# A sparse block's ReLU values rounded and split in two halves, its transposed results taken out by VectorE

## The chip, the cores and the metric

One Trainium2 chip, one of its cores. The metric is the device time of one execution in microseconds (us). The kernel before takes 928.79 us, the median of 3 runs (927.91 to 933.05).

## What is computed

Two transformer layers over four rows of 512 tokens, 128 features each. In each layer an attention with 16 heads and a feed-forward part stand behind a modulated layer norm, and each is added to x with a gate. Layer 0's feed-forward part is dense over 15 gated experts and a shared one. Layer 1's is sparse, and it alone is touched here. Cut to what matters:

```python
router_probs = softmax(xt @ Wr + br)                 # xt: 2048 tokens x 128
gates, idx = max(router_probs), argmax(router_probs) # one of E = 8 experts per token
xn = (xt - mu) * rsqrt(var + LN_EPS) * ln_g + ln_b
h = relu(einsum('te,td,edf->tf', onehot, xn, W1) + b1[idx])   # f = 512
y = einsum('te,tf,efd->td', onehot, h, W2) + b2[idx]
return y * gates
```

## The kernel before

All five engines run one program each, tied together by semaphores: TensorE (PE), VectorE (DVE), ScalarE (ACT), GpSimd (POOL) and SyncE (SP), which issues most DMAs. Each engine works strictly in the order in which its program is written. The class `Signal` (L84) is a semaphore with a list of keys: `x.by(ins, key)` lets the instruction count it up, `x.wait_ge(engine, key)` makes an engine wait for that count. `apart` (L414) is an empty instruction that holds the waits in front of it. `step` makes VectorE wait for its own instruction.

**The sparse stage.** When layer 1's attention is done, the normed tokens have been scattered to the DRAM tensor `xs`, sorted by expert into blocks of BLK = 256 tokens, each block with one expert. Eight experts with 2048 tokens need at most NBLK = 15 blocks. `block_table` (L1643) works out which block of `xs` and which expert each of the 15 has; SyncE loads all 15 blocks to `xb` (L642). Then the function `expert_blocks` of each engine goes over the blocks n = 0 to 14. A product in full precision is made of three fp32r matmuls: the value is split into a rounded half (`hi`) and the rest (`lo`), and hi x hi, hi x lo, lo x hi are added up in PSUM.

For a block n these steps follow each other, in order of the data:

1. PE `rows_in` (L1305): two transposes of `xb` to the PSUM tile `singles[0]`.
2. ACT `rounded_rows` (L987, L992) applies the norm's scale and shift and rounds to `xt_hi`; DVE `low_rows` (L1667) does the same without rounding (L1672) and subtracts (L1674) to `xt_lo`.
3. POOL (L813 to L820) copies this expert's bias columns to `b_blk` (L819) and its four weight parts, 2048 elements per partition, to `wst[n % 3]` (L820). There are three such buffers, so the copy for block n waits for `y_full` and `yt_ready` of block n - 3 (L816, L817).
4. PE `first_layer` (L1316): twelve matmuls, four chunks c of 128 hidden units times three products (L1326 to L1328), to the PSUM pair `pairs[n % 2]`, which is two banks with two chunks each. It waits for `xl_ready` and `w_here` of block n.
5. ACT `hidden` (L995): four ReLU activations of 128x256 to `hid1` (L1002), and one copy of all four, 128x1024, rounded to `hid1_hi` (L1009).
6. DVE `low_hidden` (L1676): one subtraction of 128x1024 to `hid1_lo` (L1681).
7. PE `second_layer` (L1331): twelve matmuls (L1338 to L1340) that accumulate in `p_o` or `p_m`, alternately.
8. DVE `result` (L1683): adds the bias `b2` to `yt` (L1688), which signals `yt_ready`.
9. PE `rows_out` (L1343): two transposes of `yt` to the PSUM tile `singles[1]` (L1349), signal `z_full`. ACT `result` (L1011): a copy to `yb` (L1016), signal `yb_ready`. SyncE stores `yb` to `xs` (L645).

Behind the last store POOL gathers the results by 16 indirect DMAs (L825), and DVE gates and adds them to x (L1713, L1716).

**The order on each engine**, written out by hand, in turn n of its loop:

- PE (L1355): `rows_in(n+1)`, `first_layer(n)`, `second_layer(n-1)`, `rows_out(n-2)`.
- ACT (L1020): `rounded_rows(n+1)`, `hidden(n)`, `result(n-2)`.
- DVE (L1691): `low_rows(n+1)`, `low_hidden(n)`, `result(n-1)`.
- POOL (L813): the copies for block n.
- SP (L643): the store of block n.

A signal `e_full` stands for the end of all twelve matmuls of step 4, `relu_done` for all four ReLUs, `e_hi` for the rounded copy, `e_lo` for the subtraction: one each for a block.

Of the kernel before, what the change touches and what calls it, by code (L numbers as in the profile page):

```python
# [10 lines left out]
ALU = mybir.AluOpType  # L11
# [28 lines left out]
NBLK = T * NB // 256 + E1 - 1  # L40
# [173 lines left out]
def build(nc, a, out):  # L214
    ctx = ExitStack()
    with ctx:
# [3 lines left out]
        def sig(name, keys):  # L220
            return Signal(sem(name), keys)
# [158 lines left out]
        table_ready = sig("table_ready", [0])  # L380
        xt_full, xh_ready, xl_ready = (sig(n, blocks) for n in ("xt_full", "xh_ready", "xl_ready"))
        w_here = sig("w_here", blocks)
        e_full, relu_done, e_hi, e_lo = (sig(n, blocks) for n in ("e_full", "relu_done", "e_hi", "e_lo"))
        y_full, yt_ready, z_full, yb_ready = (sig(n, blocks) for n in ("y_full", "yt_ready", "z_full", "yb_ready"))
        xb_in, yb_out = [sem(f"xb_in{i}") for i in range(NBLK)], [sem(f"yb_out{i}") for i in range(2)]
        row_done = sig("row_done", list(range(NB)))
# [24 lines left out]
        def r32(ap):  # L411
            return ap.bitcast(F32R)

        def apart(eng):  # L414
            eng.nop(nofuse=True)
# [413 lines left out]
        def _(act):  # L829
# [156 lines left out]
            def expert_blocks():  # L986
                def rounded_rows(n):  # L987
                    xt_full.wait_ge(act, n)
                    if n >= 2:
                        e_full.wait_ge(act, n - 2)  # L990
                    apart(act)
                    xh_ready.by(act.activation(r32(xt_hi[:, n % 2, :]), singles[0][:, 0:BLK], ACT.Identity,  # L992
                                               bias=cols[:, R_LNB:R_LNB + 1], scale=cols[:, R_LNG:R_LNG + 1]), n)

                def hidden(n):  # L995
                    e_full.wait_ge(act, n)
                    w_here.wait_ge(act, n)
                    if n >= 2:
                        e_lo.wait_ge(act, n - 2)
                    apart(act)  # L1000
                    for c in range(4):
                        ins = act.activation(hid1[:, n % 2, c, :], pairs[n % 2][:, c // 2, BLK * (c % 2):BLK * (c % 2) + BLK], ACT.Relu,  # L1002
                                             bias=b_blk[:, n % 3, c:c + 1])
                    relu_done.by(ins, n)
                    relu_done.wait_ge(act, n)
                    if n >= 2:
                        y_full.wait_ge(act, n - 2)
                    apart(act)
                    e_hi.by(act.activation(r32(hid1_hi[:, n % 2, :, :]), hid1[:, n % 2, :, :], ACT.Copy), n)  # L1009

                def result(n):  # L1011
                    z_full.wait_ge(act, n)
                    if n >= 2:
                        act.wait_ge(yb_out[n % 2], 16 * (n // 2))
                    apart(act)
                    yb_ready.by(act.activation(yb[:, n % 2, :, :].rearrange("p t d -> p (t d)"), singles[1][:, 0:BLK],  # L1016
                                               ACT.Copy), n)

                rounded_rows(0)
                for n in range(NBLK + 2):  # L1020
                    if n + 1 < NBLK:
                        rounded_rows(n + 1)
                    if n < NBLK:
                        hidden(n)
                    if n >= 2:
                        result(n - 2)

            for L in range(2):
                for name, b in lead_parts(L):
# [22 lines left out]
        def _(pe):  # L1052
# [251 lines left out]
            def expert_blocks():  # L1304
# [11 lines left out]
                def first_layer(n):  # L1316
                    xl_ready.wait_ge(pe, n)
                    w_here.wait_ge(pe, n)
                    if n >= 2:
                        relu_done.wait_ge(pe, n - 2)  # L1320
                    else:
                        s_taken.wait_ge(pe, (1, NSU - 2 + n))
                    for c in range(4):
                        dst = pairs[n % 2][:, c // 2, BLK * (c % 2):BLK * (c % 2) + BLK]
                        hi, lo = (r32(wst[n % 3][:, half, P * c:P * (c + 1)]) for half in range(2))
                        pe.matmul(dst, hi, r32(xt_hi[:, n % 2, :]), start=True, stop=False)  # L1326
                        pe.matmul(dst, hi, r32(xt_lo[:, n % 2, :]), start=False, stop=False)
                        ins = pe.matmul(dst, lo, r32(xt_hi[:, n % 2, :]), start=False, stop=True)  # L1328
                    e_full.by(ins, n)

                def second_layer(n):  # L1331
                    e_lo.wait_ge(pe, n)
                    if n >= 2:
                        yt_ready.wait_ge(pe, n - 2)
                    dst = (p_o, p_m)[n % 2][:, 0:BLK]
                    for c in range(4):
                        hi, lo = (r32(wst[n % 3][:, 2 + half, P * c:P * (c + 1)]) for half in range(2))
                        pe.matmul(dst, hi, r32(hid1_hi[:, n % 2, c, :]), start=(c == 0), stop=False)  # L1338
                        pe.matmul(dst, hi, r32(hid1_lo[:, n % 2, c, :]), start=False, stop=False)
                        ins = pe.matmul(dst, lo, r32(hid1_hi[:, n % 2, c, :]), start=False, stop=(c == 3))  # L1340
                    y_full.by(ins, n)
# [36 lines left out]
        def _(dve):  # L1378
# [287 lines left out]
            def expert_blocks():  # L1666
                def low_rows(n):  # L1667
                    xh_ready.wait_ge(dve, n)
                    if n >= 2:
                        e_full.wait_ge(dve, n - 2)  # L1670
                    apart(dve)
                    step(dve.tensor_scalar(singles[0][:, 0:BLK], singles[0][:, 0:BLK], cols[:, R_LNG:R_LNG + 1],  # L1672
                                           cols[:, R_LNB:R_LNB + 1], ALU.mult, ALU.add))
                    xl_ready.by(dve.tensor_tensor(r32(xt_lo[:, n % 2, :]), singles[0][:, 0:BLK], xt_hi[:, n % 2, :], ALU.subtract), n)  # L1674

                def low_hidden(n):  # L1676
                    e_hi.wait_ge(dve, n)
                    if n >= 2:
                        y_full.wait_ge(dve, n - 2)
                    apart(dve)  # L1680
                    e_lo.by(dve.tensor_tensor(r32(hid1_lo[:, n % 2, :, :]), hid1[:, n % 2, :, :], hid1_hi[:, n % 2, :, :], ALU.subtract), n)  # L1681

                def result(n):  # L1683
                    y_full.wait_ge(dve, n)
                    if n >= 2:
                        z_full.wait_ge(dve, n - 2)
                    apart(dve)
                    yt_ready.by(dve.tensor_scalar(yt[:, n % 2, :], (p_o, p_m)[n % 2][:, 0:BLK], b_blk[:, n % 3, 4:5], None, ALU.add), n)  # L1688

                low_rows(0)  # L1690
                for n in range(NBLK + 1):  # L1691
                    if n + 1 < NBLK:
                        low_rows(n + 1)
                    if n < NBLK:
                        low_hidden(n)
                    if n >= 1:
                        result(n - 1)

            for L in range(2):
                lead(L)  # L1700
# [47 lines left out]
```

## Time and profile before

| | us |
|---|---|
| median of 3 runs | 928.79 |
| lowest, highest | 927.91, 933.05 |
| the profiled execution, its own time | 935.38 |
| its span, first to last instruction | 933.7 |
| of it: the sparse stage, first block's transposes to last store (829 to 907) | 78 |
| behind it: gather and last addition (907 to 934) | 27 |

| engine | busy us in the span | share |
|---|---|---|
| PE matmul | 781.5 | 84% |
| PE weight load | 491.4 | 53% |
| DVE | 625.7 | 67% |
| ACT | 532.4 | 57% |
| POOL | 246.7 | 26% |

Shares over the whole span say little about the sparse stage, which is a twelfth of it; it has to be read by its own stretch of the trace. "Issue" in a chain or as a releaser is time in which the engine waited for nothing that the profile shows. The start of an instruction minus the start of the one before it is what it occupies its engine for; the duration in a row is somewhat longer, as two neighbours overlap. Matmul ends are modelled.

### The profile page before, as it was taken

The page shows a single profiled execution, that of the slowest core. Times are in us where ns is not written, and L with a number is a line of the kernel's source. Part 1 is how long each engine was busy: PE and PEld are TensorE (multiplying, and loading weights), DVE is VectorE, ACT ScalarE, POOL GpSimd, SP SyncE. Part 2 cuts the span into 40 slices and gives each one's busy share as a digit, 9 for nine tenths or more (in the row PEclk, how much of TensorE's full clock was granted, in tenths as well). Part 3 has the DMA queues.
Part 4 walks back from the last instruction along what each step waited for, and adds up shares of the span by engine and source line. Part 5 has one row for each costly group of instructions (what it writes and reads, how often), then busy time and mean ns, then how long its engine had stood idle before and what let it go on. Part 6 is the DMA issues. An engine that isn't in the chain of part 4 may idle for free.

```text
span 933.7 us, 12907 instructions
## 1 busy us (share of the span) xinstructions
PE 781.5 (84%) x4212; PEld 491.4 (53%) x4212; DVE 625.7 (67%) x1292; ACT 532.4 (57%) x976; POOL 246.7 (26%) x327
## 2 busy tenths in 40 slices
PE   5698878888987999999989889999999998338850
PEld 2454445545544777778767544444444442228740
DVE  3475586776663876866767696798898794435633
ACT  2355445546556677777767446667666665127740
POOL 4247654525422000000000230003202231144425
PEclk9599799999999999999999999999999997759975
DMA  6433311111100870000001121231312310021113
GB/s 177 77 65 89 69 36 21 36 36 35 34 5 1 240 211 0 1 1 1 1 11 23 25 68 35 37 79 30 91 35 43 81 25 13 0 74 46 34 34 85
DMA packets 56622, 46.84 MB, mean 50 GB/s; under 512 B 5830, under 2 KB 46619, under 8 KB 56555
## 3 DMA queue, kind: packets, MB, share of 16 engines
q1 hardware_dynamic: 55291, 43.52, 19.7%
q0 software_dynamic: 1120, 2.30, 0.9%
q8 instruction: 34, 0.56, 0.2%
q10 hardware_dynamic: 144, 0.20, 0.1%
q14 instruction: 33, 0.27, 0.1%
HBM read 14.67 MB, written 14.55 MB: 31 GB/s over the span
## 4 chain that ended last, share of the span: by engine, by line
PE 31%; DVE 8%; ACT 5%; issue 3%; POOL 2%; DMA 1%; POOLq 0%; SPq 0%; ACTq 0%; DVEq 0%
PE single L1193 7%; PE p_o L1210 6%; PE pair L1173 5%; DVE mneg L1582 3%; PE p_m L1076 2%; POOL yg L825 1%; ACT hid L1002 1%; DVE hid_lo L1681 1%; ACT hid_hi L1009 1%; ACT ring L928 1%; PE p_m L1286 1%; PE p_m L1287 1%; PE p_m L1288 1%; PE pair L1255 1%; PE pair L1257 1%
## 5 line engine op out<-in xcount | busy, mean ns | idle before, releaser
L928 ACT ACTIVATE ring<-single 128x512 f32<-128x512 f32 (+3 forms) x512 | 252.8, 518 | 193.6 <-PE single L1193 185.8
L1582 DVE TENSOR_REDUCE mneg<-pair 128x2 f32<-128x1024 f32 (+3 forms) x256 | 258.3, 1022 | 70.3 <-PE pair L1177 33.8
L1193 PE MATMUL single<-q_op,k_op 128*128 128x512 f32 (+3 forms) x512 | 216.9, 443 | 13.8 <-ACT ring L928 8.8
L1173 PE MATMUL pair<-k_op,q_op 128*128 128x512 f32 (+3 forms) x512 | 166.8, 404 | 16.9 <-DVE mneg L1582 11.3
L1193 PEld LDWEIGHTS single<-q_op,k_op 122*128 122x128 f32 (+1 forms) x512 | 97.6, 197 | 96.2 <-ACT ring L928 73.1
L1173 PEld LDWEIGHTS pair<-k_op,q_op 120*128 120x128 f32 (+1 forms) x512 | 97.6, 202 | 57.4 <-DVE mneg L1582 34.7
L1210 PE MATMUL p_o<-ring,vaug 128*9 128x512 f32 (+3 forms) x1024 | 115.6, 524 | 1.0 <-ACT ring L928 0.9
L1634 DVE TENSOR_TENSOR ring<-ring,single 128x1024 f32<-128x1024 f32 x60 | 73.3, 1221 | 47.1 <-ACT ring L957 45.6
L957 ACT ACTIVATE ring<-pair,cols 128x512 f32<-128x512 f32 x136 | 86.1, 685 | 32.7 <-PE pair L1257 27.5
L1639 DVE TENSOR_TENSOR hid_lo<-ring,hid_hi 128x1024 fp32r<-128x1024 f32 x68 | 83.3, 1225 | 23.1 <-ACT hid_hi L972 20.0
L972 ACT ACTIVATE hid_hi<-ring 128x1024 fp32r<-128x1024 f32 x68 | 72.2, 1062 | 31.7 <-issue 30.6
L731 POOL TENSOR_SCALAR_AFFINE_SELECT ring<-ring 128x256 f32<-128x256 f32 x128 | 52.3, 409 | 137.0 <-ACT ring L928 136.7
L767 POOL MEMSET k_op<- 128x2048 f32 x2 | 3.6, 1807 | 223.0 <-PE p_m L1288 223.0
L1255 PE MATMUL pair<-h,w 128*128 128x512 f32 x136 | 56.1, 412 | 0.0
L1257 PE MATMUL pair<-h,w 128*128 128x512 f32 x136 | 53.8, 396 | 0.0
L1256 PE MATMUL pair<-h,w 128*128 128x512 f32 x136 | 53.8, 395 | 0.0
L784 POOL TENSOR_TENSOR h_tok<-xn,tabs 128x512 f32<-128x512 f32 x4 | 5.1, 1276 | 153.7 <-DVE xn L1416 153.7
L1681 DVE TENSOR_TENSOR hid_lo<-hid,hid_hi 128x1024 fp32r<-128x1024 f32 x15 | 19.0, 1269 | 29.0 <-ACT hid_hi L1009 29.0
L1210 PEld LDWEIGHTS p_o<-ring,vaug 128*9 128x9 f32 x1024 | 15.3, 89 | 32.9 <-issue 19.6
L794 POOL DMA_INDIRECT xs<-xn,idx x16 | 15.7, 983 | 63.4 <-DVE idx L1559 42.5
L1002 ACT ACTIVATE hid<-pair,b_blk 128x256 f32<-128x256 f32 x60 | 23.5, 476 | 13.7 <-PE pair L1328 13.7
L1175 PE MATMUL pair<-bfc,id_bf 128*128 128x128 bf16 x128 | 31.3, 245 | 0.0
(313 smaller groups left out, 1319.8 us busy)
## 6 DMA issues: line engine op xcount, KB each, us to landing
xs<-zero SPq DMA_DIRECT2D x10, 1024.0 KB, 10.3
k_op<-hl SPq DMA_DIRECT2D x112, 64.0 KB
q_op<-hl SPq DMA_DIRECT2D x16, 256.0 KB
stage<-in_L_ffn_W_dram SPq DMA_DIRECT2D x8, 512.0 KB, 5.0
stage<-in_L_ffn_rW_dram SPq DMA_DIRECT2D x6, 512.0 KB, 5.0
q_op<-hl SPq DMA_DIRECT2D x48, 64.0 KB
xb<-xs SPq DMA_DIRECT2D x15, 128.0 KB, 2.0
xs<-yb SPq DMA_DIRECT2D x15, 128.0 KB, 1.7
```

Of the source, the lines that this page charges most:

```text
L928: exp_done.by(act.activation(ring[:, n % 8, lo:T], singles[n % 2][:, lo:T], ACT.Exp), (L, n))
L957: ins = act.activation(ring[:, k + c, :], pairs[v % 2][:, c, :], ACT.Gelu, bias=cols[:, R_B0 + 2 * u + c:R_B0 + 2 * u + c + 1])
L972: g_hi.by(act.activation(r32(hid_hi[:, i % 2, :, :]), ring[:, k:k + 2, :], ACT.Copy), i)
L1173: ins = pe.matmul(both[:, i, 0:hi], r32(qs[:, P * qt:P * (qt + 1)]), r32(ks[:, 0:hi]), start=i == 0 or L == 1 or qt >= 2, stop=L == 1)
L1193: st_full.by(pe.matmul(singles[n % 2][:, lo:T], r32(ks[:, P * kc:P * (kc + 1)]), r32(qs[:, lo:T]), start=True, stop=True), (L, n))
L1210: ins = pe.matmul(p_o[32 * j:32 * j + HD + 1, lo:T], vaug[:, (NB * L + G // NG) % 2, kc, GH * (G % NG) + j, :], ring[:, (GH * Q + j) % 8, ...
L1255: pe.matmul(pairs[v % 2][:, c, :], hi, r32(h[:, r, 0, :]), start=True, stop=False)
L1256: pe.matmul(pairs[v % 2][:, c, :], hi, r32(h[:, r, 1, :]), start=False, stop=False)
L1257: ins = pe.matmul(pairs[v % 2][:, c, :], lo, r32(h[:, r, 0, :]), start=False, stop=True)
L1582: s_taken.by(dve.tensor_reduce(mneg[:, G % 2, 2 * p:2 * p + 2, qt], both[:, :, 0:hi], axis=AX.X, op=ALU.max, negate=True), (L, m))
L1634: gated.by(dve.tensor_tensor(both, both, singles[1][:, :].unsqueeze(1).broadcast_to([P, 2, T]), ALU.mult), v)
L1639: g_lo.by(dve.tensor_tensor(r32(hid_lo[:, i % 2, :, :]), ring[:, k:k + 2, :], hid_hi[:, i % 2, :, :], ALU.subtract), i)
```

## The change

- `e_full`, `relu_done`, `e_hi` and `e_lo` get two keys for each block, (n, 0) and (n, 1).
- PE `first_layer` signals `e_full` behind the sixth and the twelfth matmul, so at each full bank of the pair.
- ACT `hidden` waits for each half by itself, makes its two ReLUs, and rounds in two instructions of 128x512 in place of one of 128x1024. It makes all four ReLUs before the first rounding; the wait for `relu_done` before each rounding is for that half.
- DVE `low_hidden` subtracts in two instructions of 128x512, each behind its own `e_hi`.
- PE `second_layer` waits for `e_lo` (n, 0) before chunk 0 and for (n, 1) before chunk 2.
- The copy of `singles[1]` to `yb` leaves ACT (`result`, an activation with Copy) and goes to DVE (`rows_out`, a `tensor_copy`) as the last step of a turn, behind `result(n-1)`; its waits, for `z_full` and for the store that last read the buffer, go with it.

```diff
-        e_full, relu_done, e_hi, e_lo = (sig(n, blocks) for n in ("e_full", "relu_done", "e_hi", "e_lo"))
+        halves = [(n, i) for n in blocks for i in range(2)]
+        e_full, relu_done, e_hi, e_lo = (sig(n, halves) for n in ("e_full", "relu_done", "e_hi", "e_lo"))
...
                 def hidden(n):
-                    e_full.wait_ge(act, n)
                     w_here.wait_ge(act, n)
                     if n >= 2:
-                        e_lo.wait_ge(act, n - 2)
-                    apart(act)
-                    for c in range(4):
-                        ins = act.activation(hid1[:, n % 2, c, :], pairs[n % 2][:, c // 2, BLK * (c % 2):BLK * (c % 2) + BLK], ACT.Relu,
-                                             bias=b_blk[:, n % 3, c:c + 1])
-                    relu_done.by(ins, n)
-                    relu_done.wait_ge(act, n)
+                        e_lo.wait_ge(act, (n - 2, 1))
+                    for i in range(2):
+                        e_full.wait_ge(act, (n, i))
+                        apart(act)
+                        for c in range(2 * i, 2 * i + 2):
+                            ins = act.activation(hid1[:, n % 2, c, :], pairs[n % 2][:, i, BLK * (c % 2):BLK * (c % 2) + BLK], ACT.Relu,
+                                                 bias=b_blk[:, n % 3, c:c + 1])
+                        relu_done.by(ins, (n, i))
                     if n >= 2:
                         y_full.wait_ge(act, n - 2)
-                    apart(act)
-                    e_hi.by(act.activation(r32(hid1_hi[:, n % 2, :, :]), hid1[:, n % 2, :, :], ACT.Copy), n)
-
-                def result(n):
-                    z_full.wait_ge(act, n)
-                    if n >= 2:
-                        act.wait_ge(yb_out[n % 2], 16 * (n // 2))
-                    apart(act)
-                    yb_ready.by(act.activation(yb[:, n % 2, :, :].rearrange("p t d -> p (t d)"), singles[1][:, 0:BLK],
-                                               ACT.Copy), n)
+                    for i in range(2):
+                        relu_done.wait_ge(act, (n, i))
+                        apart(act)
+                        e_hi.by(act.activation(r32(hid1_hi[:, n % 2, 2 * i:2 * i + 2, :]), hid1[:, n % 2, 2 * i:2 * i + 2, :], ACT.Copy), (n, i))
...
                         ins = pe.matmul(dst, lo, r32(xt_hi[:, n % 2, :]), start=False, stop=True)
-                    e_full.by(ins, n)
+                        if c % 2:
+                            e_full.by(ins, (n, c // 2))
...
                 def second_layer(n):
-                    e_lo.wait_ge(pe, n)
...
                     for c in range(4):
+                        if c % 2 == 0:
+                            e_lo.wait_ge(pe, (n, c // 2))
...
                 def low_hidden(n):
-                    e_hi.wait_ge(dve, n)
                     if n >= 2:
                         y_full.wait_ge(dve, n - 2)
-                    apart(dve)
-                    e_lo.by(dve.tensor_tensor(r32(hid1_lo[:, n % 2, :, :]), hid1[:, n % 2, :, :], hid1_hi[:, n % 2, :, :], ALU.subtract), n)
+                    for i in range(2):
+                        e_hi.wait_ge(dve, (n, i))
+                        apart(dve)
+                        part = slice(2 * i, 2 * i + 2)
+                        e_lo.by(dve.tensor_tensor(r32(hid1_lo[:, n % 2, part, :]), hid1[:, n % 2, part, :], hid1_hi[:, n % 2, part, :],
+                                                  ALU.subtract), (n, i))
...
+                def rows_out(n):
+                    z_full.wait_ge(dve, n)
+                    if n >= 2:
+                        dve.wait_ge(yb_out[n % 2], 16 * (n // 2))
+                    apart(dve)
+                    yb_ready.by(dve.tensor_copy(yb[:, n % 2, :, :].rearrange("p t d -> p (t d)"), singles[1][:, 0:BLK]), n)
+
                 low_rows(0)
-                for n in range(NBLK + 1):
+                for n in range(NBLK + 2):
                     if n + 1 < NBLK:
                         low_rows(n + 1)
                     if n < NBLK:
                         low_hidden(n)
-                    if n >= 1:
+                    if 1 <= n <= NBLK:
                         result(n - 1)
+                    if n >= 2:
+                        rows_out(n - 2)
```

The other lines of the diff name the half (n - 2, 1) where before they named block n - 2, and end ACT's loop at NBLK.

## Rows read from the trace of the kernel before

**Rows 1.** Stretches: us, busy PE PEld DVE ACT POOL, PEclk, DMA: stage, ten blocks.

```profile
829.00:907.00 78.00, 59.45 (x420) 54.40 (x420) 38.69 (x60) 50.73 (x105) 25.90 (x25) 0.89 0.16 50
851.08:894.39 43.31, 36.26 (x278) 33.17 (x279) 25.39 (x41) 33.25 (x70) 20.24 (x20) 1.00 0.10 31
```

**Rows 2.** Waits, 829 to 907: who waited for whom, us in total, times, longest.

```profile
POOL b_blk L819 <- DVE yt L1688: 39.4, 12, 12.3
```

**Rows 3.** Timeline of one turn: start us, us, engine line op tiles xcount [idle before].

```profile
852.87 1.57 ACT L1002 ACTIVATE hid<-pair,b_blk 128x256 f32<-128x256 f32 x4 [1.60 <-PE pair L1328]
854.54 1.06 ACT L1009 ACTIVATE hid_hi<-hid 128x1024 fp32r<-128x1024 f32 x1
855.74 1.23 DVE L1681 TENSOR_TENSOR hid_lo<-hid,hid_hi 128x1024 fp32r<-128x1024 f32 x1 [2.36 <-ACT hid_hi L1009]
856.88 0.48 DVE L1688 TENSOR_SCALAR yt<-p_m,b_blk 128x256 f32<-128x256 f32 x1
857.56 0.19 POOL L819 COPY b_blk<-b_cols 128x5 f32 x1 [2.88 <-DVE yt L1688]
857.69 1.89 POOL L820 CAST wst<-w 128x2048 fp32r x1
857.85 0.42 DVE L1674 TENSOR_TENSOR xt_lo<-single,xt_hi 128x256 fp32r<-128x256 f32 x1
859.68 0.36 PE L1326 MATMUL pair<-xt_hi,wst 128*128 128x256 f32 x1 [0.53 <-issue]
861.25 0.19 POOL L819 COPY b_blk<-b_cols 128x5 f32 x1 [1.68 <-DVE yt L1688]
861.47 1.57 ACT L1002 ACTIVATE hid<-pair,b_blk 128x256 f32<-128x256 f32 x4 [1.46 <-PE pair L1328]
```

**Rows 4.** Timeline: two subtractions beside weight copies.

```profile
849.09 1.89 POOL L820 CAST wst<-w 128x2048 fp32r x1
850.50 1.56 DVE L1681 TENSOR_TENSOR hid_lo<-hid,hid_hi 128x1024 fp32r<-128x1024 f32 x1 [0.81 <-ACT hid_hi L1009]
859.42 1.24 DVE L1681 TENSOR_TENSOR hid_lo<-hid,hid_hi 128x1024 fp32r<-128x1024 f32 x1 [1.14 <-ACT hid_hi L1009]
```

**Rows 5.** Timeline of PE without a stall: first layer, second layer.

```profile
851.08 0.36 PE L1326 MATMUL pair<-xt_hi,wst 128*128 128x256 f32 x1 [0.54 <-issue]
852.58 0.28 PE L1338 MATMUL p_m<-hid_hi,wst 128*128 128x256 f32 x1
```

**Rows 6.** Groups by form, whole span: busy us, mean ns, idle before.

```profile
L1002 ACT ACTIVATE hid<-pair,b_blk 128x256 f32<-128x256 f32 x60 | 23.5, 476 | 13.7 <-PE pair L1328 13.7
L907 ACT ACTIVATE h<-hF 128x512 fp32r<-128x512 f32 x4 | 2.5, 620 | 0.0
L1716 DVE TENSOR_TENSOR x<-x,yg 128x512 f32<-128x512 f32 x4 | 2.8, 691 | 0.1
L1384 DVE COPY cols<-p_m 128x85 f32<-128x85 f32 x1 | 0.2, 248 | 0.0
```

**Rows 7.** Timeline of the first blocks.

```profile
833.38 0.41 PE L1328 MATMUL pair<-xt_hi,wst 128*128 128x256 f32 x1
835.19 1.57 ACT L1002 ACTIVATE hid<-pair,b_blk 128x256 f32<-128x256 f32 x4 [2.02 <-PE pair L1328]
848.28 0.48 DVE L1688 TENSOR_SCALAR yt<-p_m,b_blk 128x256 f32<-128x256 f32 x1
```

**Rows 8.** Busy time by stretch: block 0's second layer; the dense stage.

```profile
839.30:842.20 2.90, 2.90 (x14) 2.90 (x15) 1.95 (x3) 1.58 (x3) 0.00 (x0) 0.51 0.34 101
500.00:520.00 20.00, 20.00 (x88) 15.83 (x87) 15.40 (x13) 15.14 (x20) 0.00 (x0) 1.00 0.02 7
```

**Rows 9.** Timeline and chain of the last block.

```profile
894.39 0.36 PE L1326 MATMUL pair<-xt_hi,wst 128*128 128x256 f32 x1 [1.05 <-issue]
900.31 0.39 PE L1338 MATMUL p_o<-hid_hi,wst 128*128 128x256 f32 x1 [2.62 <-DVE hid_lo L1681]
902.98 0.48 DVE L1688 TENSOR_SCALAR yt<-p_o,b_blk 128x256 f32<-128x256 f32 x1 [2.33 <-PE p_o L1340]
905.21 1.71 DMA xs<-yb
```

More of the change, by code:

```diff
@@ L989, in rounded_rows @@
                     if n >= 2:
-                        e_full.wait_ge(act, n - 2)
+                        e_full.wait_ge(act, (n - 2, 1))
                     apart(act)
@@ L995, in hidden @@
                 def hidden(n):
-                    e_full.wait_ge(act, n)
                     w_here.wait_ge(act, n)
                     if n >= 2:
-                        e_lo.wait_ge(act, n - 2)
-                    apart(act)
-                    for c in range(4):
-                        ins = act.activation(hid1[:, n % 2, c, :], pairs[n % 2][:, c // 2, BLK * (c % 2):BLK * (c % 2) + BLK], ACT.Relu,
-                                             bias=b_blk[:, n % 3, c:c + 1])
-                    relu_done.by(ins, n)
-                    relu_done.wait_ge(act, n)
+                        e_lo.wait_ge(act, (n - 2, 1))
[6 more added lines that the diff above has]
+                        relu_done.by(ins, (n, i))
                     if n >= 2:
                         y_full.wait_ge(act, n - 2)
-                    apart(act)
-                    e_hi.by(act.activation(r32(hid1_hi[:, n % 2, :, :]), hid1[:, n % 2, :, :], ACT.Copy), n)
-                def result(n):
-                    z_full.wait_ge(act, n)
-                    if n >= 2:
-                        act.wait_ge(yb_out[n % 2], 16 * (n // 2))
-                    apart(act)
-                    yb_ready.by(act.activation(yb[:, n % 2, :, :].rearrange("p t d -> p (t d)"), singles[1][:, 0:BLK],
-                                               ACT.Copy), n)
+                    for i in range(2):
+                        relu_done.wait_ge(act, (n, i))
+                        apart(act)
+                        e_hi.by(act.activation(r32(hid1_hi[:, n % 2, 2 * i:2 * i + 2, :]), hid1[:, n % 2, 2 * i:2 * i + 2, :], ACT.Copy), (n, i))
                 rounded_rows(0)
-                for n in range(NBLK + 2):
+                for n in range(NBLK):
                     if n + 1 < NBLK:
                         rounded_rows(n + 1)
[L1023 to L1026, printed above, removed]
+                    hidden(n)
             for L in range(2):
@@ L1319, in first_layer @@
                     if n >= 2:
-                        relu_done.wait_ge(pe, n - 2)
+                        relu_done.wait_ge(pe, (n - 2, 1))
                     else:
@@ L1669, in low_rows @@
                     if n >= 2:
-                        e_full.wait_ge(dve, n - 2)
+                        e_full.wait_ge(dve, (n - 2, 1))
                     apart(dve)
```

## The prediction

> **What bounds the kernel now.** I read the busy times by stretch first. The sparse stage is 78.0 us long, and ten of its fifteen blocks take 43.31 us between two starts of the first layer, 4.33 each, with PE busy for 36.26 and ACT for 33.25 [rows 1]. No engine is full, so a loop of waits bounds the stage.
>
> The chain of waits puts most of the stage down to the ReLUs, the rounding and the subtraction, but before every second first layer it shows PE idle for 0.53 with "issue" as the releaser [rows 3]. That is a wait which the profile couldn't name. The table of waits and the timeline name it. POOL's copy of a block's weights waits for `yt` all 12 times that it can, 39.4 us in all [rows 2], and PE's first layer starts 0.10 after the copy ends (857.69 + 1.89 = 859.58, then 859.68) [rows 3]. VectorE makes that `yt`, which belongs to the block before, only behind this block's subtraction. So the loop is, from block n's ReLUs: 1.67 to the rounding, 1.20 to the subtraction, 1.14 to `yt`, 0.81 to the weight copy, 1.89 for it, 0.10 to the first layer of block n+2, 1.79 to its ReLUs. The sum is 8.60, and 861.47 - 852.87 is 8.60 [rows 3]. Even and odd blocks each run such a loop, hence 4.30 a block.
>
> A second thing is in the timeline. The subtraction has two inputs in SBUF and is 1.23 long when POOL is quiet. Where it started at 850.50 under a weight copy that ended at 850.98 it took 1.56 and ended at 852.06, 1.08 behind the copy [rows 4]. The one at 859.42 ended at 860.66, again 1.08 behind the copy of rows 3. One more of the fifteen was stretched in the same way; POOL's copy was 1.89 throughout. So a subtraction can't get further under a weight copy than if it had begun 0.15 before the copy's end.
>
> **The change part by part.**
>
> *First layer and ReLUs by halves.* Twelve matmuls take 1.50 [rows 5], so a half is signalled about 0.72 earlier: first layer to first ReLU becomes 1.79 - 0.72 = 1.07. The ReLUs overlap: (1.57 - 0.48) / 3 = 0.365 from start to start, 0.48 being a single one [rows 3, 6]. The second half's matmuls end about when the third ReLU may start, so the four keep 1.57.
>
> *Rounding in halves.* The first half's ReLUs are done long before, so the rounding needn't wait for the last one and starts at 4 x 0.365 = 1.46, not 1.67. A half's price isn't shown for this tile: 0.53 (half of 1.06) from below, 0.62 from an SBUF copy of 128x512 [rows 6] from above. I take 0.60 long, 0.50 apart. With the 0.14 of the hand-over that rows 3 show, the first subtraction may start at 1.46 + 0.60 + 0.14 = 2.20.
>
> *Subtraction in halves.* Half of 1.23 is 0.62; a 128x512 one took 0.69 [rows 6]. I take 0.69; the whole one occupies 1.14 of its 1.23, so a half occupies 0.60. The second half starts at 2.80 (its input is there at 2.70), `yt` at 3.40, where before it was 4.01 behind the ReLUs.
>
> The loop is then 1.07 + 3.40 + 0.81 + 1.89 + 0.10 = 7.27 for two blocks, 3.64 a block. **But the weight copy now stands in the way.** It runs from 0.81 to 2.70 behind each `yt`; the next block's first half can't count as begun before 2.55, the second follows at 3.15, the next `yt` at 3.75. That is more than 3.64, so I take 3.75 a block. The same sum with the whole subtraction gives 2.55 + 1.14 = 3.69, which is the short step of the kernel before (`b_blk` at 857.56 and at 861.25 [rows 3], with the subtraction of rows 4 in between).
>
> The Trainium skill ("SBUF — State Buffer", section "Who interferes with whom") says that a VectorE instruction with two SBUF inputs and a GpSimd one that reads SBUF exclude each other, and the later one blocks fully. By that rule the half would run its whole length behind the copy, so a block would be about 0.26 longer (an estimate), some 4.0, and the change would give 2.6 less; the trace agrees that the two collide, but shows 1.08 left of 1.23.
>
> *The copy to `yb` on VectorE.* On ACT its removal gives nothing by itself: ACT was idle 1.60 and 1.46 before the ReLUs of this loop [rows 3]. On VectorE it costs between 0.25 (85 columns from PSUM) and 0.48 (`yt`, 256 columns from PSUM) [rows 3, 6]; I take 0.40. It is queued behind `yt`, with the next block's norm and subtraction behind it. `xt_lo` was done 1.39 behind `yt` (858.27) and will be at 1.8, when the weight copy still has 0.9 to run. So the weight copy hides it; were that cover gone, ten blocks would pay 4.0. Its new wait on `z_full` is over some 1.7 earlier, as PE's transposes out follow second layer n-1 directly; the store that it waits for is two blocks old, about 7.5. SP's stores and POOL's copies move with it and are not lengthened. PE's own work, 3.63 a block [rows 1], fits in 3.75, closely.
>
> *The start.* Half of block 0's first layer is done at 833.8 [rows 7], so its first two ReLUs go before 835.19; the roundings start at 835.92 and 836.42, the subtractions at 836.65 and 837.25, the second layer behind the first of them (0.69 and a hand-over) at 837.4. Before, it ran from 839.3 to 842.2 at a granted clock of 0.51, the lower level of 1.2 GHz, behind an idle PE [rows 8]; now there is next to no gap, and I take the upper level, which PE had reached. `xt_lo` of block 2 comes at 838.8, its first layer at 839.1. Block 1: ReLUs 837.4 (ACT comes from block 2's norm), subtraction 839.56, `yt` 840.76, weight copy 841.57 to 843.46. Block 2: subtraction ready at 842.5, held to 843.31, `yt` at 844.51, where it was 848.28 [rows 7]. **Gain 3.8.**
>
> *Ten blocks.* 43.31 against 37.5. **Gain 5.8.**
>
> *The end.* From the last first layer to the last store's landing it was 905.21 + 1.71 - 894.39 = 12.53 [rows 9]. Now the last second layer starts at 1.07 + 2.20 + 0.74 = 4.0 (it was 900.31 - 894.39 = 5.92), takes 1.8 to `yt` at the upper clock (it was 2.67, largely at the lower one, behind 2.62 of idle PE; now the gap is about 0.8), and 3.7 more (it was 3.94). That is 9.5. **Gain 3.0.**
>
> The sum is 12.6. The profiled execution takes 935.38 with a span of 933.7, 6.6 over the median of the runs; it would become 922.8, the span 921.1. All that is saved lies in a stage that both have, so I take the same 12.6 from the median: 928.79 - 12.6 = 916.2.
>
> **The rivals.**
>
> *The halves slip past the weight copy.* If a short subtraction isn't held as the long one was, the waits' loop of 7.27 rules: 36.4 for ten blocks, 0.8 more at the start, so 14.5 in all, 914.3. For it: only few rows show the hold. Against it: two of them end 1.08 behind the copy to the hundredth. Chance 0.13.
>
> *The hand-overs eat the halves.* If each added wait drains its engine, the second half and `yt` start 0.23 later each (0.69 + 0.14 in place of 0.60): 4.2 a block, 1.2 for ten, some 3.3 at the start and 2.6 at the end, 7 in all, 921.8. Against it: `yt` started 0.09 before the subtraction ended, with a satisfied wait and an `apart` between them [rows 3]. Chance 0.10, nearly half of it lost in what can't be told from no change.
>
> *Slower: PE's clock.* PE would be busy for 3.63 of every 3.75. If the chip then grants the lower level through the stage, a layer with its transposes takes the 2.90 of block 0's second layer [rows 8], and a block of two layers some 6.0: with 1.7 more for each of fifteen blocks, 25 slower, 954. It decides as soon as a block takes over 4.6, that is when the lower level holds for a good part of the blocks. Against it: in the dense stage PE is busy 20.00 of 20.00 at a granted clock of 1.00 [rows 8], and the ten blocks now run at 1.00 [rows 1]. Chance 0.05.
>
> **How the numbers follow.** My forecast has 0.72, and 916.2. Its unknown prices move it from 915 (halves at their lower bounds, upper clock everywhere) to 919 (4.0 a block, or the lower clock at the start and the end, 1 us each). With the first two rivals and the scatter of a median of runs that lie 5 apart, the range is 912.5 to 921.8. A measurement here can tell about 0.5%, 4.6 us, from no change. Faster by more: 0.88 (0.70 + 0.13 + 0.05). Within it: 0.07. Slower: 0.05.
>
> **What would show it.** Right: first layers 3.75 apart from block 4 on, with no long and short step in turn; the first half of the subtraction longer than the second, ending 0.54 behind a weight copy; PE's first layer still 0.1 behind the end of a weight copy; block 0's second layer at a granted clock of 1.00; ACT idle longer than before; the last store landing near 894. Wrong: steps under 3.7 with equal halves (first rival), gaps between the halves on VectorE with no weight copy beside them (second), a granted clock of 0.5 in the middle of the stage (third), or VectorE idle in front of its copy to `yb`, waiting for PE, which would break the sum at the cover that I gave that copy.

## The result and the profile after

| | us |
|---|---|
| kernel before, median of 4 runs (lowest to highest) | 928.35 (927.83 to 933.05) |
| changed kernel, median of 4 runs (lowest to highest) | 915.89 (914.68 to 916.99) |
| ratio, 95% interval | 0.986 (0.9828 to 0.9892) |
| profiled execution of the changed kernel: time, span | 916.05, 914.1 |

The change gives 12.5 us, 1.4%; 916.2 was forecast. Two later measurements of the same pair gave 8.0 and 10.0 (experiments 8 and 11). The spans of the two profiled executions differ by more, 933.7 - 914.1 = 19.6. Of that, 9.15 lies ahead of the sparse stage: its first transposes start at 829.27 before and at 820.12 after, though nothing ahead of them was changed. In other profiled executions of kernels of this study they start anywhere from 821 to 829. So the stage is compared by its own clock, from here on: from those first transposes (T0) to the first `yt`, to the last `yt`, and to the start of the gather behind the last store.

The table of waits of the changed kernel, 829 to 896:

```profile
POOL b_blk L820 <- DVE yt L1685: 30.3, 12, 10.9
ACT hid L1004 <- DVE hid_lo L1677: 9.6, 12, 1.5
PE pair L1318 <- issue: 4.2, 12, 0.8
```

POOL still waits for `yt` before all 12 weight copies, 30.3 us where it was 39.4 [rows 2]. In the second line the releaser is misnamed: the ReLUs of block n wait for the subtraction of block n - 2, over long before, and for PE's first half. In this kernel that half and the running subtraction happen to end together; in experiment 3, where they don't, the ReLUs start 1.14 behind the first layer (856.94 - 855.80) and 0.67 before the subtraction ends. The busy times of nine blocks and of block 0's second layer (us; busy of PE, PEld, DVE, ACT, POOL; PE clock; DMA):

```profile
838.22:872.12 33.90, 31.57 (x252) 29.70 (x253) 28.14 (x55) 27.75 (x64) 18.22 (x18) 1.00 0.11 36
828.20:831.00 2.80, 2.77 (x22) 2.66 (x23) 2.04 (x4) 2.80 (x8) 0.00 (x0) 1.00 0.34 105
```

Nine blocks in 33.90 are 3.77 each, where ten took 4.33 each [rows 1]. PE was busy 84% of the time [rows 1] and is now at 93%. VectorE went from 0.59 (25.39 / 43.31) to 0.83. The second row is where PE ran at the lower level before [rows 8].

One turn of the loop, from the timelines of the engines put together in order of time:

```profile
854.25 0.47 DVE L1685 TENSOR_SCALAR yt<-p_o,b_blk 128x256 f32<-128x256 f32 x1
854.65 0.41 DVE L1692 COPY yb<-single 128x256 f32<-128x256 f32 x1
854.98 0.54 DVE L1666 TENSOR_SCALAR single<-single,cols 128x256 f32<-128x256 f32 x1
855.05 1.89 POOL L821 CAST wst<-w 128x2048 fp32r x1
855.55 0.42 DVE L1668 TENSOR_TENSOR xt_lo<-single,xt_hi 128x256 fp32r<-128x256 f32 x1
856.58 1.51 DVE L1677 TENSOR_TENSOR hid_lo<-hid,hid_hi 128x512 fp32r<-128x512 f32 x2 [0.60 <-ACT hid_hi L1012]
857.05 0.36 PE L1318 MATMUL pair<-xt_hi,wst 128*128 128x256 f32 x1 [0.24 <-issue]
858.01 0.47 DVE L1685 TENSOR_SCALAR yt<-p_m,b_blk 128x256 f32<-128x256 f32 x1
858.17 1.57 ACT L1004 ACTIVATE hid<-pair,b_blk 128x256 f32<-128x256 f32 x4 [0.68 <-DVE hid_lo L1677]
859.61 1.16 ACT L1012 ACTIVATE hid_hi<-hid 128x512 fp32r<-128x512 f32 x2
```

Read it as three links. The weight copy starts 0.80 behind `yt` (855.05 - 854.25) and ends at 856.94. The two subtraction halves end at 856.58 + 1.51 = 858.09, 1.15 behind the copy. `yt` starts 0.08 before that. 0.80 + 1.89 + 1.15 - 0.08 = 3.76, and the two `yt` are 3.76 apart. PE's first layer starts 0.11 behind the copy's end, as before, but no longer sets the pace (experiment 3). From the same timelines, a pair at block 0 with no weight copy beside it, the pair of block 2, and a first half alone with the weight copy before it:

```profile
827.49 1.29 DVE L1677 TENSOR_TENSOR hid_lo<-hid,hid_hi 128x512 fp32r<-128x512 f32 x2 [2.34 <-ACT hid_hi L1012]
833.38 2.12 DVE L1677 TENSOR_TENSOR hid_lo<-hid,hid_hi 128x512 fp32r<-128x512 f32 x2 [0.34 <-ACT hid_hi L1012]
858.82 1.90 POOL L821 CAST wst<-w 128x2048 fp32r x1
860.34 0.92 DVE L1677 TENSOR_TENSOR hid_lo<-hid,hid_hi 128x512 fp32r<-128x512 f32 x1 [0.60 <-ACT hid_hi L1012]
```

The pair is 1.29 long when POOL is quiet, 1.51 in a turn, and 2.12 where its input came early. The first half alone ends at 861.26, 0.54 behind the copy's end at 860.72. That is how an engine held by another looks in a profile: no wait, no "issue", only an instruction that is longer than its equals.

The end of the stage, from the chain of waits (start, us, what):

```profile
880.32 0.36 PE p_o L1332
882.12 0.17 DVE yt L1685
882.52 0.42 DVE yb L1692
883.08 0.43 PE single L1343 x2
883.63 0.44 DVE yb L1692
884.19 3.14 DMA xs<-yb
887.87 1.00 POOL yg L826
```

The last first layer starts at 876.19. The last store takes 3.14, where it took 1.71 [rows 9].

### The profile page after: what moved, and what is told of

It reads as the page before. It is cut to its first block and busy times, and to the rows that moved or that the text cites. A ratio compares the mean times of both kernels' runs of the same rounds, so it can differ in the third digit from the quotient of the medians.

```text
span 914.1 us, 12982 instructions
## 1 busy us (share of the span) xinstructions
PE 766.9 (84%) x4212; PEld 483.1 (53%) x4212; DVE 634.3 (69%) x1322; ACT 527.9 (58%) x976; POOL 246.6 (27%) x327
## 5 line engine op out<-in xcount | busy, mean ns | idle before, releaser
L1185 PE MATMUL single<-q_op,k_op 128*128 128x512 f32 (+3 forms) x512 | 213.4, 435 | 14.6 <-ACT ring L929 9.3
L1165 PE MATMUL pair<-k_op,q_op 128*128 128x512 f32 (+3 forms) x512 | 162.9, 396 | 17.3 <-DVE mneg L1576 12.0
L1165 PEld LDWEIGHTS pair<-k_op,q_op 120*128 120x128 f32 (+1 forms) x512 | 94.9, 197 | 58.0 <-DVE mneg L1576 32.9
L1202 PE MATMUL p_o<-ring,vaug 128*9 128x512 f32 (+3 forms) x1024 | 113.4, 515 | 1.0 <-ACT ring L929 0.9
L1677 DVE TENSOR_TENSOR hid_lo<-hid,hid_hi 128x512 fp32r<-128x512 f32 x30 | 23.0, 804 | 11.6 <-ACT hid_hi L1012 10.1
L1167 PE MATMUL pair<-bfc,id_bf 128*128 128x128 bf16 x128 | 30.3, 236 | 0.0
```

Source lines behind the costliest of these rows:

```text
L1165: ins = pe.matmul(both[:, i, 0:hi], r32(qs[:, P * qt:P * (qt + 1)]), r32(ks[:, 0:hi]), start=i == 0 or L == 1 or qt >= 2, stop=L == 1)
L1185: st_full.by(pe.matmul(singles[n % 2][:, lo:T], r32(ks[:, P * kc:P * (kc + 1)]), r32(qs[:, lo:T]), start=True, stop=True), (L, n))
L1202: ins = pe.matmul(p_o[32 * j:32 * j + HD + 1, lo:T], vaug[:, (NB * L + G // NG) % 2, kc, GH * (G % NG) + j, :], ring[:, (GH * Q + j) % 8, ...
```

## The experiments

Each is measured beside the kernel before on the same chip: 1 to 4 on one chip, 5 to 8 on a second, 9 to 12 on a third. In total time the variants of the changed kernel lie so close together that most of their intervals overlap; they are told apart by the stage. "Steps" are the times between two starts of `yt`. Experiments 3, 4, 7 and 12 share one preparation, four weight buffers in place of three, and as many buffers for the bias columns (room was free behind `h` and in the last 1 KB of `at_op`).

### 1. Only the copy to `yb`, on the kernel before

The first two lines are ACT's loop, the last two VectorE's, where the copy follows `yt` of block n - 1.

```diff
-                    if n >= 2:
-                        result(n - 2)
...
+                    if n >= 2:
+                        rows_out(n - 2)
```

> The kernel before, with only the copy to yb moved from ACT to VectorE. Theory (the loop through ReLUs, rounding, subtraction, yt and the weight copy sets the stage, and a weight copy holds up a subtraction): neither ACT's time nor the 0.4 us on VectorE is in the loop, since the copy lies under the weight copy, so within 1 us of the kernel before and still about 8.6 us for two blocks. Rival 1 (ACT's load counts): 15 x 0.26 us = 4 us faster. Rival 2 (VectorE's queue counts, the copy pushes norm and subtraction back): 0.33 us a block, 5 us slower.

Measured: 928.46 (12 runs) against 929.06 (17 runs), ratio 1.0 (0.9984 to 1.0015). The steps are 4.05 and 4.55 in turn, 8.61 for two blocks against 8.60. The copy gives nothing and costs nothing.

Its profile holds something else. Block 0's second layer ran at the upper clock although PE had been idle longer in front of it (2.36) than in the kernel before (2.10):

```profile
833.33 0.39 PE L1327 MATMUL p_o<-hid_hi,wst 128*128 128x256 f32 x1 [2.36 <-DVE hid_lo L1670]
```

And the busy times of that stretch:

```profile
833.33:835.50 2.17, 2.17 (x18) 2.17 (x19) 1.21 (x3) 1.72 (x4) 0.00 (x0) 1.00 0.41 118
```

So the lower level at the start of the profile before [rows 8] wasn't a property of that kernel, but of that execution.

### 2. Only the halves

The changed kernel with the `yb` copy back on ACT.

> The changed kernel, with the copy to yb back on ACT, so the halves alone. Theory: all of the gain is in the halves; ACT has 0.6 us idle in each block, so the same as the changed kernel within 1 us (about 916), 3.77 us from one first layer to the next. Rival (the copy had to leave ACT, as its wait for PE's transposes would stand in front of the next block's norm): 0.2 to 0.4 us a block more, 3 to 6 us slower than the changed kernel.

Measured: 917.73 (915.89 to 921.57), ratio 0.9892 (0.9869 to 0.9916). The steps are 3.77 and the stage from first to last `yt` is 50.57 against 50.47. The halves are the whole of the change.

### 3. Four weight buffers

```diff
-                if n >= 3:
-                    y_full.wait_ge(pool, n - 3)
-                    yt_ready.wait_ge(pool, n - 3)
+                if n >= 4:
+                    y_full.wait_ge(pool, n - 4)
+                    yt_ready.wait_ge(pool, n - 4)
```

> The changed kernel with a fourth weight buffer, so that the weight copy for block n waits for block n-4 and is out of the loop of waits; each copy still starts about 0.8 us behind a yt. Theory (the hold): the subtraction's second input waits for the weight copy whatever block that copy is for, so 3.77 us a block stay and the time is within 1 us of the changed kernel (916). Rival (the loop of waits through the weight copy alone sets the time, the hold costs nothing): PE becomes the bound at about 3.5 us a block, 12 blocks x 0.25 = 3 us faster, 913.

Measured: 918.72 (917.34 to 923.92), ratio 0.9901 (0.9877 to 0.9924). The steps stay at 3.77. In the timeline of a turn:

```profile
854.57 1.89 POOL L822 CAST wst<-w 128x2048 fp32r x1
855.41 2.20 DVE L1678 TENSOR_TENSOR hid_lo<-hid,hid_hi 128x512 fp32r<-128x512 f32 x2
857.53 0.47 DVE L1686 TENSOR_SCALAR yt<-p_o,b_blk 128x256 f32<-128x256 f32 x1
```

Everything ahead of the subtraction is earlier (PE's first layer starts at 855.80, 0.66 before the weight copy that runs then has ended, so it doesn't wait for it), it has no idle time in front of it, and all of that goes into its length, 2.20. It ends at 857.61, again 1.15 behind the copy (856.46). With the first layer's wait for weights gone and the pace the same, the hold is shown to be the bound of the changed kernel.

### 4. The weight copy started earlier

Experiment 3, with POOL's copy released by the end of a subtraction:

```diff
+                    e_lo.wait_ge(pool, (n - 2, 1))
```

> As the one with four buffers, and the weight copy for block n waits also for the second half of the subtraction of block n-2 (e_lo), so it starts about 0.45 us behind yt's start in place of 0.8 and is over before the next subtraction. Theory (the hold): the next subtraction is no longer held, about 3.5 us a block (then PE's own work is the bound), 12 x 0.25 = 3 us faster than the changed kernel, 913. Rival (no hold, the waits alone): no faster than the one with four buffers, both 913 or both 916.

Measured: 914.73 (912.8 to 917.22), ratio 0.9858 (0.9836 to 0.9879). Run once more as experiment 9:

> The kernel with the early copy again, beside the changed kernel on the same chip. Theory: 3.51 us a block in place of 3.77 and one step of 2.9 at the start, 3.5 us faster than the changed kernel. Rival (the part of the runs that stands before the sparse stage differs by more than that between programs): no difference that the intervals show.

914.92 (912.36 to 917.78), ratio 0.9851 (0.9816 to 0.9885). The steps are 3.48 and 3.54 in turn:

```profile
854.00 1.90 POOL L823 CAST wst<-w 128x2048 fp32r x1
855.83 1.29 DVE L1679 TENSOR_TENSOR hid_lo<-hid,hid_hi 128x512 fp32r<-128x512 f32 x2 [0.61 <-ACT hid_hi L1014]
```

The copy ends at 855.90, the subtraction starts 0.07 before that and is 1.29 long: not held any more. What bounds the pace now is not PE's own work, as my expectation had it: experiment 12 runs at 3.31. It is the loop through the weight copy, at its new release point. PE's first layer again starts 0.10 behind the copy's end, at 856.00. From one end of a subtraction to that of two blocks later it is 0.43 to the weight copy, 1.90 for it, 0.10 to the first layer, 1.13 to the ReLUs, 1.44 to the rounding, 0.73 to the subtraction and 1.29 for it: 7.02, or 3.51 a block.

### 5. Halves without the early signal

```diff
-                        if c % 2:
-                            e_full.by(ins, (n, c // 2))
+                        if c == 3:
+                            e_full.by(mid, (n, 0))
+                            e_full.by(ins, (n, 1))
```

`mid` is the matmul before the last. The ReLUs thus wait for the whole first layer, as before the change.

> The changed kernel, but both halves of e_full are signalled only at the end of the first layer (by the last two matmuls), so rounding and subtraction are in halves and the ReLUs start as late as before. Theory: the ReLUs come 0.55 to 0.6 us later, the loop of waits is 7.30 + 0.57 = 7.87 us for two blocks, more than the hold's 2 x 3.77, so 3.93 us a block, and 0.16 x 12 + 1 at start and end = 3 us slower than the changed kernel. Rival (the early signal is worth nothing, since the hold or the weight copy sets the time anyway): the same as the changed kernel.

Measured: 921.82 (920.01 to 923.27), ratio 0.9931 (0.9904 to 0.9957). The steps are 3.81 and 4.09 in turn, 3.95 in the mean, where the loop of waits gave 3.93.

### 6. The early signal without the halves behind it

ReLUs by halves, rounding and subtraction whole.

> The changed kernel, but the rounding and the subtraction are whole again (128x1024) and the ReLUs still go by halves. Theory: yt comes 4.01 us behind the ReLUs in place of 3.38, the loop is 1.12 + 4.01 + 2.80 = 7.93 us for two blocks, 3.97 us a block, 0.20 x 12 + 1 to 2 at start and end = 4 us slower than the changed kernel. Rival (the split of rounding and subtraction only helps PE, whose second layer may start sooner, and PE isn't the bound): the same as the changed kernel.

Measured: 921.29 (920.41 to 922.76), ratio 0.9919 (0.9895 to 0.9943). The steps are 3.82 and 4.05 in turn, 3.94 in the mean, where the loop of waits gave 3.97. In the middle of the stage of both experiments no subtraction is stretched (1.29 the pair, 1.23 the whole one), so there the loop alone sets the pace. In total time neither can be told from the changed kernel of experiment 8 on the same chip (920.36); in the steps they can. Each half of the change alone gives about two thirds of its 0.54 a block (4.31 to 3.95 or 3.94). Both together give less than the sum, 0.54 in place of 0.73, since the hold catches them at 3.77.

### 7. The weight copy a block ahead

Experiment 3 with five buffers for the bias columns, and POOL's copy of block n released by `e_lo` of block n - 3, a full block earlier than in experiment 4.

> Four weight buffers and five for the bias columns; the weight copy for block n waits for the end of the subtraction of block n-3 (and for the second layer of block n-4), so it lies right behind a subtraction, as in the one with the early copy, but is a block ahead of its need. Theory: neither the weight copy nor the hold is in a loop any more; PE's own work (about 3.4 us a block) is the bound where the early copy left 3.51; 12 x 0.08 = 1 us faster than that one and 4 us faster than the changed kernel. Rival (the early copy was already at PE's bound): the same as the early copy, 3.5 us a block.

Measured: 917.62 (913.85 to 920.94), ratio 0.9877 (0.985 to 0.9904). Run once more as experiment 10:

> The kernel with the copy a block ahead again, beside the changed kernel. Theory: PE is the bound at 3.47 us a block, 4 us faster than the changed kernel and within 1 us of the early copy. Rival: as for the early copy.

916.39 (913.07 to 920.92), ratio 0.9866 (0.9832 to 0.9901). The medians lie 2.9 and 1.5 above those of the early copy (the first on another chip), where 1 us below was expected, but the intervals overlap. From first to last `yt` it is 0.6 faster. The steps are 3.47:

```profile
854.29 0.47 DVE L1688 TENSOR_SCALAR yt<-p_o,b_blk 128x256 f32<-128x256 f32 x1
854.80 1.89 POOL L824 CAST wst<-w 128x2048 fp32r x1
856.16 1.68 DVE L1680 TENSOR_TENSOR hid_lo<-hid,hid_hi 128x512 fp32r<-128x512 f32 x2
```

The hold is back: the pair is 1.68 long and ends at 857.84, 1.15 behind the copy (856.69). The same sum gives the pace: 0.51 from `yt` to the copy, 1.89, 1.15, less 0.08, is 3.47. PE is busy 34.73 of 35.00 from 845 to 880, and 35.00 of 35.00 from 838 to 873, and I first read that as PE being the bound. Experiment 12 shows that it wasn't; its waits were only too short to leave gaps between matmuls whose ends are modelled. The starts show them: the transposes of the next block start 0.35 behind those of `yt`, and the first layer 0.17 behind them, where in experiment 12 it is 0.22 and 0.14. The 0.16 between the two sums is the 0.16 between the steps.

### 8 and 11. The changed kernel again, beside the others

> The changed kernel itself, beside the others on the same chip: 0.986 of the kernel before, as in its first measurement; first layers 3.77 us apart.

> The changed kernel again, to be compared with the others of this call: 9 to 12 us under the kernel before; first layers 3.77 us apart.

Measured: 920.36 (916.86 to 923.74) against 928.38, ratio 0.9914 (0.989 to 0.9938); and 919.06 (914.62 to 921.17) against 929.03, ratio 0.9889 (0.9856 to 0.9922). So the gain is 8.0 and 10.0 here, after 12.5 in the first measurement. The stage is the same to 0.1 from first to last `yt` in all three profiled executions (50.47, 50.53, 50.50). So the scatter of the medians seems to lie outside of the stage, or in its end; only one execution of each is profiled, and the others aren't seen.

### 12. The weight copy on top of the subtraction

Experiment 7 with another release. It was made to bring out the hold at its worst: POOL's copy starts when the subtraction does.

```diff
-                    e_lo.wait_ge(pool, (n - 3, 1))
+                    e_hi.wait_ge(pool, (n - 3, 0))
```

> As the copy a block ahead, with one wait moved: the weight copy starts with the first half of a subtraction (it waits for that block's first e_hi) in place of behind its end. It is still a block ahead of its need. Theory (the hold): the second half of each subtraction can't end before the copy does, yt comes 1.5 to 1.8 us later, the loop through the norm's subtraction becomes the bound, about 4.1 us a block, some 7 us slower than the copy a block ahead. Rival (only the loop of waits through the weight copy ever counted): 3.47 us a block, no difference.

Measured: 915.41 (908.87 to 917.57), ratio 0.9856 (0.9818 to 0.9894). The expectation fell, with its sign: the steps are 3.31, the shortest of the study. The timeline of a turn:

```profile
854.32 0.36 PE L1321 MATMUL pair<-xt_hi,wst 128*128 128x256 f32 x1
854.32 1.29 DVE L1680 TENSOR_TENSOR hid_lo<-hid,hid_hi 128x512 fp32r<-128x512 f32 x2 [0.37 <-ACT hid_hi L1015]
854.53 0.54 POOL L823 COPY b_blk<-b_cols 128x5 f32 x1 [0.46 <-ACT hid_hi L1015]
855.01 2.37 POOL L824 CAST wst<-w 128x2048 fp32r x1
857.28 0.38 PE L1346 MATMUL single<-cst,yt 128*128 128x128 f32 x2
857.49 0.38 PE L1308 MATMUL single<-cst,xb 128*128 128x128 f32 x2
857.63 1.29 DVE L1680 TENSOR_TENSOR hid_lo<-hid,hid_hi 128x512 fp32r<-128x512 f32 x2 [0.37 <-ACT hid_hi L1015]
```

The busy times of ten blocks:

```profile
838.00:871.00 33.00, 33.00 (x281) 33.00 (x281) 28.96 (x61) 30.94 (x71) 25.28 (x18) 1.00 0.12 41
```

Now POOL's instructions are the long ones. Its small copy takes 0.54 in place of 0.19 and its weight copy 2.37 in place of 1.89, while the pair keeps its 1.29. So the collision works in both directions: of the two, the one that started first runs on, and the later one pays. The step that failed in my expectation was that POOL's copy would get in between the two halves and hold the second. The small copy did end near the boundary of the halves (855.07), but the weight copy was 0.48 longer (2.37 - 1.89), most of the 0.60 that the pair still had to run, and POOL has that much to spare: it is done at 857.38, 0.25 before the next pair. At 3.31 PE's matmuls follow one another without an idle bracket, PE is busy 33.00 of 33.00, and the starts leave no gap as they do in experiment 7. I take this as PE's bound for the stage; no run here tried for less.

### The stage in all versions

From the starts of the instructions in each profiled execution: T0 to the first `yt`, from there to the last, from there to the gather, and the sum.

```
version                           T0-yt0  yt0-yt14  yt14-gather   sum   step
before                             13.01    60.70      4.20      77.91  3.70/4.90
1  copy to yb only                 12.96    58.57      4.32      75.85  4.05/4.55
5  no early signal                 12.04    52.94      5.08      70.06  3.81/4.09
6  no halves behind the ReLUs      12.21    54.21      4.32      70.74  3.82/4.05
2  halves only                     11.53    50.57      3.73      65.83  3.77
the change                         11.53    50.47      5.75      67.75  3.77
8  the change                      11.53    50.53      4.03      66.09  3.77
11 the change                      11.50    50.50      4.22      66.22  3.77
3  four buffers                    11.52    49.50      6.06      67.08  3.77
4  copy earlier                    11.52    46.73      4.42      62.67  3.48/3.54
9  copy earlier                    11.53    46.75      4.04      62.32  3.48/3.55
7  copy a block ahead              11.55    46.14      5.46      63.15  3.47
10 copy a block ahead              11.44    46.13      5.74      63.31  3.47
12 copy on top                     11.53    44.06      4.04      59.63  3.31
```

The last version is the best of all: its stage is 6.5 shorter than that of the changed kernel in experiments 8 and 11, and its median is 3.7 below that of experiment 11, on the same chip. In total time the two can't be told apart surely, since their intervals against the kernel before overlap (0.9818 to 0.9894, and 0.9856 to 0.9922); in the stage they can.

## Why the prediction was right

*The loop before.* Held. With the halves the pace falls by 0.54 a block, and with one part of them taken away the same loop gave 3.93 and 3.97 ahead of experiments 5 and 6, which ran at 3.95 and 3.94. In experiment 3, where the first layer no longer waits for weights, the pace is no longer tied to that loop.

*The floor under the new loop.* This step decides the size, and it held. My waits' sum gave 3.64 a block and the hold 3.75; measured were 3.77, with the half ending 0.54 behind the copy, as forecast, and the pair 1.15. The first rival, that short halves slip past, is out. The Trainium skill ("SBUF — State Buffer", section "Who interferes with whom") says that such a pair contends for a shared path, that the path is locked for one of them at a time, and that issue order decides who blocks; the words "fully blocks" stand there for VectorE's two-port modes. The order is shown in both directions, by experiments 3 and 12. In length the measurement decides: the held half ended 0.54 behind the copy, not its full 0.69, so that about 0.15 of it lay beside the copy; why, no run shows. My estimate by the rule, some 4.0 a block, doesn't come out of my own terms: 2.70 + 0.60 + 0.60 behind `yt` is 3.90, so 0.15 more than 3.75 and not 0.26. The 3.77 measured is below both. No term of the forecast rests on it.

*The price of a half.* 0.69 was taken for a subtraction and 1.29 for the pair: 1.29 was measured. ReLU to rounding was 1.44 (1.46 taken) and first layer to ReLU 858.17 - 857.05 = 1.12 (1.07 taken). The second rival, hand-overs that eat the halves, is out.

*The copy to `yb`.* Taken at 0.40 and hidden; it is 0.41 long and its removal from the change moves nothing (experiment 2). In the changed kernel its cover is the weight copy: `xt_lo` is done at 855.97, and by the prediction's rule the subtraction couldn't begin to count before 856.79, 0.15 ahead of the copy's end.

*PE's clock.* 1.00 in the nine blocks at 93% busy. The slower rival is out.

*The start.* 3.8 forecast, 3.7 measured: from T0 to the second `yt` is 19.01 before and 15.30 after. But part of it is luck. Some 1.1 of it is the lower clock of block 0's second layer in the profile before (839.29 to 841.97, against 833.33 to 834.87 in experiment 1), and there the idle time was longer. Against experiment 1, whose T0 to second `yt` is 12.96 + 4.55 = 17.51, the gain at the start is 2.2.

*Ten blocks.* 5.8 forecast; the first layers of blocks 4 and 14 are 876.19 - 838.22 = 37.97 apart, so 5.3. Nine steps are 3.77, the tenth 4.07. There POOL's small copy starts 0.97 behind `yt` and not 0.67, the same 0.30 for which the kernel before has a 4.01 among its short steps. I hadn't asked why the last step of the stretch was odd.

*The end.* 3.0 forecast, 1.4 measured: 887.33 - 876.19 = 11.14, where it was 12.53. My terms were 4.0, 1.8 and 3.7. Measured: 4.13 to the second layer, 1.80 to `yt`, 2.07 to the store's issue and 3.14 for the store. Only the store is off. With the 1.71 of experiment 8 the last term is 3.78.

*The sum.* By the profiled executions 3.7 + 5.3 + 1.4 = 10.4, or 11.8 with an ordinary store, against 12.6. The medians say 12.5, 8.0 and 10.0 in three measurements. So 916.2 met 915.89 a little better than the terms deserve: the profile before held a lower clock at its start and a longer end (last `yt` step 2.81 against 2.09 in experiment 1), and I took what it showed as the kernel's. The stage of experiment 1 less that of experiment 11 is 9.6, and for me that is the best value of the gain, though it is one execution against one. The path was right; that the total came out within 0.4 us was in part luck.

*Of the things to look for*, two were off. I wrote that ACT would be idle longer. It is busy 27.75 of 33.90, 82%, against 77% before, and idle 0.68 ahead of its ReLUs, where it was 1.46 and 0.23 in turn. ACT's copy, 0.36 to 0.38 long in the kernel before, was gone, but the block itself became 0.56 shorter. And the last store was to land near 894, by the clock of the profile before, so 65 behind T0; it landed at 887.33, 67.2 behind T0, of which 1.4 is the long store. The first changed no term; the second is the missing gain of *Ten blocks* and *The end*.

## What to carry to other kernels

Before a chain is shortened, look for an instruction that is longer than its equals beside work of another engine: no wait names it, and it can be the next floor. Where VectorE and GpSimd collide, place the work so that the engine with time to spare starts last; a fourth weight buffer and another release point took 0.46 a block, after the halves had taken 0.54. An engine at 99 or 100% busy isn't yet the bound, if its idle pieces can hide in modelled ends. And don't take a clock or a transfer time for the kernel's own when one profiled execution shows it once.

## What was not expected of the hardware

The collision of a VectorE subtraction with two SBUF inputs and a GpSimd copy goes by order of start, with POOL paying 0.35 on a copy of 0.19 and 0.48 on one of 1.89 when it comes second. VectorE's instructions with at most one SBUF input kept their lengths under the copy: the norm's 0.54 and the 0.42 to `xt_lo` in the changed kernel, the 0.41 of the copy to `yb` in experiment 4 (from 853.89).

Near the end of the stage a store of the same 128 KB landed in 1.7 in most cases, in 3.14 here, 3.95 in experiment 3, 3.62 in 10, 2.85 in 7 and 2.49 in 5. In the stretches of the three longest the queues' table lists a packet of instruction fetching beside the store, in those of experiments 5 and 7 none, and none in that of experiment 8 (1.7). For the changed kernel, 884 to 887.4:

```profile
q8 instruction: 1, 0.02, 1.7%
xs<-yb SPq DMA_DIRECT2D x1, 128.0 KB, 3.1
```

So the packet goes with the longest ones, but stores come late without it too. What delays them stays open; it wasn't tried.

PE's granted clock fell in one execution after 2.10 of idle time and not in another after 2.36. What decides it stays open.
